# A convolution block: last product in four column tiles, its sum through DRAM, and the squares of queries and keys on GpSimd

## The chip, the core and the metric

The kernel runs on one core of one Trainium2 chip. The metric is device time in microseconds (us), the median of several runs. PE is TensorE, PEld its weight load, DVE is VectorE, ACT is ScalarE, POOL is GpSimd, SP is SyncE, which issues most of the DMAs here.

## The reference, cut to what matters

Three stages follow each other on x of 32 samples x 96 channels x 1024 positions: a convolution block (below, with C = 96, 8 heads of 12), causal attention with 6 heads of 16, and a feed-forward layer with quantized activations. Only the first stage and the projection of queries, keys and values that hangs on it are touched. `xs` is x after a group norm over 3 channels.

```python
xn = (xs - mu) / sqrt(var + EPS) * ln_g + ln_b
mid = silu(xn @ fc1_w + fc1_b) @ fc2_w + fc2_b          # 96 -> 384 -> 96
q, k, v = xs @ qkv_w                                    # per head of 12
q = q / norm(q);  k = k / norm(k)
attn = einsum('bhld,bhle->bhde', k, v)
o = 0.5 * v + 1.0 / pi * einsum('bhld,bhde->bhle', q, attn)
o = o / norm(o) + mid
x1 = x + (o @ proj_w + proj_b)
# then: t = tokens of x1;  q, k, v = ln(t) @ Wq, Wk, Wv   (causal attention)
```

## The kernel before

`prepare` loads and folds the weights once: `w["fc2"]` is fc2_w times proj_w, `w["out_bias"]` the bias of the sum. `conv_block` then takes the 32 samples one after the other through all its steps, as a pipeline: each engine has a `body(i, ...)` that in step i does one part for each of up to eight samples, `on(s)` meaning "the part that lags s samples". The order of the statements in each `body` is the order of the engine's work, and semaphores named after results tie the engines together. `_pipeline` unrolls the bodies. In one step:

- **TensorE** turns XN (L581), makes K'V (L588), waits for `a_ready`, makes the group mean G (L594), the QKV product of sample i-1 in eight tiles of 128 tokens x 384 (L604, two banks of `pq` in turn), the product M (L609), turns O-hat (L615), fc1's chunk 0 (L572, `hidden(i, 0)`), fc2 and proj of sample i-3 into `po` (L627, L631: two halves of 512 columns, K of 3 x 128 and 96), fc1's chunks 1 and 2 (L572), the attention projection of sample i-4 from X1 (L644, eight tiles), and the query product U (L651). `hidden` for chunk 1 waits until ScalarE has taken chunk 0 out of `pf` by its SiLU. K'V, M and G lie in `po`, which fc2 writes later.
- **ScalarE** squares O (L513), copies the turned XN (L516), takes roots (L519, L523, with a load of the root table), copies the QKV product out (L527, eight copies), squares its last 96 columns (L530) and queries and keys (L532), copies the turned O-hat (L535), rounds to bf16 (L539), roots again (L542, L546 and L548; these wait for the sums of the norms), loads the SiLU table and applies SiLU six times (L553), and takes the attention projection out: a copy (L561) and a square (L562) for each of eight tiles.
- **VectorE** sums a_squares (L388), masks the attention matrix (L391), sums O's squares and inverts the roots (L394, L398), copies G and makes the group variance (L402, L405), copies M (L409), scales queries and keys of sample i-5 to `a_qk` (L413, L416), makes the third bf16 part of sample i-6 (L421), sums the squares (L425, L426), scales XN and K-hat (L430 to L435), takes statistics of the next x (L442), adds x to fc2's result (L450, with x loaded a second time as XR), and at the end makes O (L462) and the normed x, XS (L471).
- **GpSimd** scales O (L482), waits until the packed rows of sample i-7 have been stored (`rows_stored`), makes the values' part (L489), a rest (L494), the scaled queries and values (L498), and a second rest (L503).
- **SP** issues in this order, first waiting for XS: x of the next sample (L365), x again (L368), the store of X1 (L371), the store of 1.5 MB packed rows (L374). All are on one queue.

The attention projection of sample i-4 reads X1 from SBUF one step after VectorE has made it. The feed-forward stage has a product in the tiled form that the change brings in (L1122).

Of the kernel before, what the change touches and what calls it, by code (L numbers as in the profile page):

```python
# [8 lines left out]
ALU = mybir.AluOpType  # L9
# [4 lines left out]
L = SIDE * SIDE  # L14
# [33 lines left out]
def _constants(nc, ctx):  # L48
# [15 lines left out]
    w["proj"] = sb("proj", [C, C])  # L64
    w["out_bias"] = sb("out_bias", [C, 1])
# [9 lines left out]
def prepare(nc, w, A):  # L75

    ctx = ExitStack()
    with ctx:
# [3 lines left out]
        def sem(name):  # L82
# [15 lines left out]
        projb = sb("projb", [C, 1])  # L98
# [17 lines left out]
            (w["proj"][:, :], A["L0_conv_proj_w"]),  # L116
# [13 lines left out]
            (projb[:, :], A["L0_conv_proj_b"].rearrange("(n a) -> n a", a=1)),  # L130
# [4 lines left out]
        with nc.Block() as block:  # L135
# [43 lines left out]
            def _(dve):  # L179
# [24 lines left out]
                link(dve.tensor_tensor(w["out_bias"][:, :], bank[4][0:C, 0:1], projb[:, :], ALU.add))  # L204
# [26 lines left out]
            def _(pe):  # L231
# [8 lines left out]
                pe.matmul(bank[4][0:C, 0:1], w["proj"][:, :], fc2b[:, :], start=True, stop=True)  # L240
# [7 lines left out]
                for k in range(CHUNKS):  # L248
                    pe.matmul(bank[0][:, k * C:(k + 1) * C], fc2_t[:, k * P:(k + 1) * P], w["proj"][:, :],
                              start=True, stop=True)  # L250
# [32 lines left out]
def conv_block(nc, w, x_in, x1, rows):  # L283
# [9 lines left out]
    with ExitStack() as ctx:  # L293
# [6 lines left out]
        XR = sb("x_again", [C, 2, L])  # L300
# [26 lines left out]
        OHT = sb("o_hat_t", [C, L])  # L327
        HT = sb("hidden_t", [P, 2, CHUNKS, L])
        AQKV = sb("a_qkv", [P, 2, TILES, 3 * C])
# [5 lines left out]
        AR1 = sb("a_rest", [P, TILES * HEADS, 2, HD])  # L335
        PK = sb("packed", [P, 2, TILES * HEADS, PACK], U32)

        def part(slot, n):
# [8 lines left out]
        x1_stored = [sem(f"x1_stored{i}") for i in range(2)]  # L347
        rows_stored = [sem(f"rows_stored{i}") for i in range(2)]
        names = ("bn_parts bn_done mv_ready g_done g_copied gn_var gn_std gn_scale xs_ready qkv_psum qkv_copied "
                 "squares norm_sums norm_roots norm_scales khat_ready xn_ready qv_ready kv_done a_ready m_done "  # L350
                 "m_ready xnt_psum xnt_ready fc1_psum hid_ready u_done o_ready o_squares o_sums o_roots o_scale "
                 "ohat_ready oht_psum oht_ready out_done x1_ready a_psum a_copied a_sums a_roots a_scale qk_ready "
                 "v_ready high_ready rest_ready mid_ready low_ready").split()
        S = {n: sem(n) for n in names}

# [3 lines left out]
        with nc.Block() as block:  # L359
            @block.sync  # L360
            def _(sp):
                def body(i, r, lap, on):
# [3 lines left out]
                    if on(3):  # L366
                        _above(sp.wait_ge, S["x1_ready"], i - 4)
                        sp.dma_start(XR[:, (r + 1) % 2, :], x_in[i - 3]).then_inc(xr_loaded[(r + 1) % 2], 16)  # L368
                    if on(4):
                        sp.wait_ge(S["x1_ready"], i - 3)  # L370
                        sp.dma_start(x1[i - 4], X1[:, r, :]).then_inc(x1_stored[r], 16)  # L371
                    if on(7):
# [3 lines left out]
                                     ).then_inc(rows_stored[(r + 1) % 2], 16)  # L376
                _pipeline(sp, body, BATCH, 8, 2, ahead=1)
                for r in range(2):
                    sp.wait_ge(x1_stored[r], 16 * (BATCH // 2))
                    sp.wait_ge(rows_stored[r], 16 * (BATCH // 2))  # L380

            @block.vector
            def _(dve):
                def body(i, r, lap, on):
                    q = (r + 1) % 2
                    if on(5):
                        dve.wait_ge(S["a_copied"], TILES * (i - 4))
# [4 lines left out]
                    if on(3):  # L392
# [5 lines left out]
                        dve.reciprocal(OI[:, :], OR[:, :]).then_inc(S["o_scale"], 1)  # L398
                    if on(0):
# [45 lines left out]
                    if on(3):  # L445
                        dve.wait_ge(S["out_done"], i - 2)
                        dve.wait_ge(xr_loaded[q], _dmas(lap, r, 3, 2))
                        _above(dve.wait_ge, x1_stored[q], _dmas(lap, r, 5, 2))
                        _above(dve.wait_ge, S["a_psum"], TILES * (i - 4))
                        dve.scalar_tensor_tensor(out=X1[:, q, :], in0=po[0:C, :], scalar=w["out_bias"][:, 0:1],  # L450
                                                 in1=XR[:, q, :], op0=ALU.add, op1=ALU.add).then_inc(S["x1_ready"], 1)
# [24 lines left out]
            def _(pool):  # L476
                def body(i, r, lap, on):
                    q = (r + 1) % 2
                    if on(3):
# [4 lines left out]
                                           _bcast(OI[:, :], 2, LIN_DIM), ALU.mult).then_inc(S["ohat_ready"], 1)  # L484
                    if on(5):
# [22 lines left out]
            def _(act):  # L508
                def body(i, r, lap, on):
# [14 lines left out]
                    if on(1):  # L524
# [7 lines left out]
                        act.activation(SQ[:, :, 0:2 * C], QKV[:, q, :, 0:2 * C], ACT.Square).then_inc(S["squares"], 1)  # L532
                    if on(3):
                        act.wait_ge(S["oht_psum"], i - 2)
                        act.activation(OHT[:, :], pt[0:C, :], ACT.Copy).then_inc(S["oht_ready"], 1)  # L535
# [31 lines left out]
            def _(pe):  # L567
# [7 lines left out]
                def body(i, r, lap, on):  # L575
# [10 lines left out]
                    if on(2):  # L586
# [741 lines left out]
```

## Time and profile before

| what | us |
|---|---|
| median of 3 runs | 3130.85 (3129.27 to 3132.96) |
| the profiled execution | 3126.59 |
| its span, first to last instruction | 3124.9 |
| convolution block within it | to about 1090 |
| 28 full samples of the block | 859.37, 30.69 each |

Busy times over the span: TensorE 2841.3 us, VectorE 2173.1, ScalarE 2052.4, GpSimd 1393.8. The shares are means over three stages with different limits. To read the change, one takes one sample of the block and follows each engine through it in the timeline view, where a gap is printed with the engine that ended it.

### The profile page before, as it was taken

The page shows a single profiled execution, that of the slowest core. Times are in us where ns is not written, and L with a number is a line of the kernel's source. Part 1 is how long each engine was busy: PE and PEld are TensorE (multiplying, and loading weights), DVE is VectorE, ACT ScalarE, POOL GpSimd, SP SyncE. Part 2 cuts the span into 40 slices and gives each one's busy share as a digit, 9 for nine tenths or more (in the row PEclk, how much of TensorE's full clock was granted, in tenths as well). Part 3 has the DMA queues.
Part 4 walks back from the last instruction along what each step waited for, and adds up shares of the span by engine and source line. Part 5 has one row for each costly group of instructions (what it writes and reads, how often), then busy time and mean ns, then how long its engine had stood idle before and what let it go on. Part 6 is the DMA issues. An engine that isn't in the chain of part 4 may idle for free. (4 is left out here: it accounts for less than half of the span.)

```text
span 3124.9 us, 85427 instructions
## 1 busy us (share of the span) xinstructions
PE 2841.3 (91%) x28774; PEld 1733.4 (55%) x28966; DVE 2173.1 (70%) x4403; ACT 2052.4 (66%) x3943; POOL 1393.8 (45%) x2063
## 2 busy tenths in 40 slices
PE   3899999999998589999999999999999979999883
PEld 2445455454544256666666666666666645555541
DVE  3565665656566378888898898889888935455542
ACT  2677777777776357777777777777777745666561
POOL 0143444444343444434444444443444413577778
PEclk9999999999999789999999999999999989999996
DMA  1113232322222367655556565565655523234434
GB/s 32 41 51 107 71 106 70 106 80 96 97 93 82 112 125 117 120 111 119 115 115 119 112 119 116 115 120 111 119 115 115 117 67 96 81 98 125 126 98 107
DMA packets 919803, 315.97 MB, mean 101 GB/s; under 512 B 848257, under 2 KB 904354, under 8 KB 919714
## 3 DMA queue, kind: packets, MB, share of 16 engines
q1 hardware_dynamic: 916258, 313.98, 42.4%
q8 instruction: 57, 0.93, 0.1%
q10 hardware_dynamic: 3456, 0.79, 0.1%
q14 instruction: 32, 0.26, 0.0%
HBM read 113.35 MB, written 99.88 MB: 68 GB/s over the span
## 5 line engine op out<-in xcount | busy, mean ns | idle before, releaser
L939 DVE TENSOR_REDUCE at_unit_max<-at_ps_queries 128x1 f32<-128x512 f32 (+3 forms) x2304 | 1121.1, 548 | 119.7 <-PE at_ps_queries L831 97.5
L905 ACT ACTIVATE at_probs<-at_ps_keys 128x512 f32<-128x512 f32 x1344 | 738.5, 596 | 244.7 <-PE at_ps_keys L845 216.7
L831 PE MATMUL at_ps_queries<-at_turned 96*128 96x512 bf16 (+3 forms) x2304 | 688.0, 330 | 64.3 <-DMA at_turned<-at_spread 31.8
L845 PE MATMUL at_ps_keys<-at_turned 128*128 128x128 bf16 (+3 forms) x3264 | 593.8, 268 | 2.9 <-ACT at_probs L905 2.4
L845 PEld LDWEIGHTS at_ps_keys<-at_turned 128*128 128x128 bf16 x3456 | 255.4, 97 | 241.1 <-ACT at_probs L905 122.6
L865 PE MATMUL at_ps_values<-at_probs,at_v 128*32 128x128 f32 x10752 | 373.4, 276 | 0.5 <-ACT at_probs L905 0.5
L799 POOL TENSOR_TENSOR at_tick<-at_one 128x1 f32<-128x1 f32 x192 | 37.1, 193 | 705.5 <-ACT at_diag_probs L905 460.2
L834 PE MATMUL at_ps_queries<-mask_queries,ident_bf 128*128 128x128 bf16 x1536 | 338.8, 221 | 0.0
L865 PEld LDWEIGHTS at_ps_values<-at_probs,at_v 128*32 128x32 f32 x10752 | 270.6, 109 | 42.3 <-ACT at_probs L905 1.3
L1189 POOL TENSOR_SCALAR ff_hidden<-ff_hidden 128x1024 f32<-128x1024 f32 x90 | 246.9, 2769 | 63.6 <-ACT ff_hidden L1147 63.6
L831 PEld LDWEIGHTS at_ps_queries<-at_turned 96*128 96x128 bf16 x2304 | 217.5, 98 | 100.7 <-DMA at_turned<-at_spread 32.9
L482 POOL TENSOR_TENSOR cb_o_hat<-cb_o,cb_o_scale 128x768 f32<-128x768 f32 x32 | 48.0, 1501 | 402.0 <-DVE cb_o_scale L398 402.0
L905 ACT ACTIVATE at_diag_probs<-at_ps_keys 128x512 f32<-128x512 f32 x384 | 208.5, 595 | 13.0 <-PE at_ps_keys L845 4.5
L801 POOL TENSOR_SCALAR_AFFINE_SELECT at_diag_probs<-at_diag_probs 128x1024 f32<-128x1024 f32 x192 | 209.6, 1091 | 0.0
L604 PE MATMUL cb_ps_qkv<-w_lin,cb_xs 96*128 96x384 f32 x512 | 198.9, 521 | 7.0 <-ACT cb_qkv L527 4.5
L644 PE MATMUL cb_ps_qkv<-w_attn,cb_x 96*128 96x384 f32 x512 | 198.2, 512 | 5.8 <-ACT cb_a_squares L562 4.3
L1122 PE MATMUL ff_ps_out<-ff_hidden,w 128*32 128x256 f32 x2160 | 138.7, 410 | 62.3 <-POOL ff_hidden L1189 23.6
L572 PE MATMUL cb_ps_hidden<-cb_xn_t,fc 96*128 96x512 f32 x384 | 185.7, 614 | 8.4 <-ACT cb_hidden_t L553 8.4
L834 PEld LDWEIGHTS at_ps_queries<-mask_queries,ident_bf 128*128 128x128 bf16 x1536 | 151.9, 99 | 72.5 <-issue 0.8
L462 DVE SCALAR_TENSOR_TENSOR cb_o<-cb_q_norm_v,cb_ps_hidden 128x768 f32<-128x768 f32 x32 | 30.5, 953 | 210.2 <-PE cb_ps_hidden L651 210.2
L627 PE MATMUL cb_ps_out<-cb_hidden_t,fc 128*96 128x512 f32 x384 | 176.6, 595 | 0.0
L1056 PE MATMUL ff_ps_hidden<-ff_xn_t,w 97*128 97x512 f32 x360 | 172.0, 600 | 1.1 <-ACT ff_xn_t L1154 1.1
(199 smaller groups left out, 4896.4 us busy)
## 6 DMA issues: line engine op xcount, KB each, us to landing
qkv_rows<-cb_packed SPq DMA_DIRECT2D x32, 1536.0 KB, 8.3
at_stacks<-qkv_rows SPq DMA_DIRECT2D x192, 256.0 KB, 3.2
cb_x<-in_x_dram SPq DMA_DIRECT2D x32, 384.0 KB, 3.7
cb_x_again<-in_x_dram SPq DMA_DIRECT2D x32, 384.0 KB, 4.5
x_after_conv<-cb_x SPq DMA_DIRECT2D x32, 384.0 KB, 5.0
attention_rows<-at_att SPq DMA_DIRECT2D x384, 32.0 KB, 2.1
ff_att_rows<-attention_rows SPq DMA_DIRECT2D x32, 384.0 KB, 3.7
ff_x<-x_after_conv SPq DMA_DIRECT2D x32, 384.0 KB, 4.7
```

What stands on the lines that cost most here:

```text
L572: pe.matmul(pf[:, a * BANK:(a + 1) * BANK], w["fc1"][:, k * P:(k + 1) * P], XNT[:, a * BANK:(a + 1) * BANK], start=True, stop=True).then_i ...
L604: pe.matmul(pq[:, (t % 2) * BANK:(t % 2) * BANK + 4 * C], XS[:, q, t * P:(t + 1) * P], w["w_lin"][:, :], start=True, stop=True).then_inc(S ...
L627: pe.matmul(po[0:C, half], w["fc2"][:, k, :], HT[:, q, k, half], start=(k == 0), stop=False)
L644: pe.matmul(pq[:, (t % 2) * BANK:(t % 2) * BANK + 4 * C], X1[:, r, t * P:(t + 1) * P], w["w_attn"][:, :], start=True, stop=True).then_inc( ...
L801: pool.affine_select(out=blocks, in_=blocks, compare_op=ALU.is_ge, fill=0.0, base=0, pattern=[[0, TILES], [1, P]], channel_multiplier=-1). ...
L831: mm = pe.matmul(pq[:, u % QBANKS, 0:n], QT[0:STACK, slot, qb * P:(qb + 1) * P], KT[0:STACK, slot, k0:k0 + n], start=True, stop=True)
L834: mm = pe.matmul(pq[:, u % QBANKS, n - P:n], w["ident_bf"][:, :], w["mask_queries"][:, :], start=False, stop=True, skip_group_check=True)
L845: mm = pe.matmul(pk[:, bank_k, c0:c0 + n * P], KT[:, slot, kb * P:(kb + 1) * P], QT[:, slot, q0 * P:(q0 + n) * P], start=(c0 == 0), stop=True,
L865: mm = pe.matmul(pv[row:row + VW, col:col + P], V[:, slot, kb, :], probs[:, c0:c0 + P], start=(v == 0), stop=True, skip_group_check=True)
L905: act.activation(probs, pk[:, (slot * NU + k) % KBANKS, :], ACT.Exp, scale=scale).then_inc(S["probs"], 1)
L939: dve.tensor_reduce(MX[:, r % 2, qb, k0 // BANK:k0 // BANK + 1], pq[:, u % QBANKS, 0:n], AX.X, ALU.max).then_inc(S["unit_max"], 1)
L1189: pool.tensor_scalar(Y1[:, s % SLOTS, k, :], Y1[:, s % SLOTS, k, :], LIMIT, None, ALU.min).then_inc(S["h_ready"], 1)
```

## The change

It does six things in the convolution block.

1. fc2 and proj go into `po` in four column tiles: tile g holds 32 channels (three blocks b of them in turn) and a quarter of the tokens, 256 columns; 4 K-chunks x 3 x 4 = 48 matmuls of 32 output rows. The bias becomes a 97th row of `w["proj"]` against a row of ones in OHT. The result lies as 128 partitions x 768.
2. VectorE's addition of x is a plain addition of 128x768 into X1Q. XR is loaded, and X1Q stored, in that layout, by four DMAs each. X1 (96x1024), which the attention projection reads, is loaded back from DRAM, issued behind the store of the rows, once the store of X1Q has landed.
3. The squares of queries and keys move from ScalarE to GpSimd, behind L482 and ahead of L489.
4. In TensorE's order, the wait for `a_ready`, G, and with it M come behind the QKV product. On VectorE the copy of M comes ahead of the copy of G and the group variance.
5. The attention projection is copied out whole (384 columns), and its squares are one operation of 128x768 behind the eight copies.
6. A root of one column, whose result isn't used, ends ScalarE's step.

```diff
@@ sync
-                        sp.dma_start(XR[:, (r + 1) % 2, :], x_in[i - 3]).then_inc(xr_loaded[(r + 1) % 2], 16)
+                        for q in range(4):
+                            sp.dma_start(XR[q * QP:(q + 1) * QP, (r + 1) % 2, :, :], quarters(x_in[i - 3])[q]
+                                         ).then_inc(xr_loaded[(r + 1) % 2], 16)
                     if on(4):
                         sp.wait_ge(S["x1_ready"], i - 3)
-                        sp.dma_start(x1[i - 4], X1[:, r, :]).then_inc(x1_stored[r], 16)
+                        for q in range(4):
+                            sp.dma_start(quarters(x1[i - 4])[q], X1Q[q * QP:(q + 1) * QP, r, :, :]
+                                         ).then_inc(x1_stored[r], 16)
                     if on(7):
...
+                    if on(4):
+                        sp.wait_ge(x1_stored[r], 4 * _dmas(lap, r, 4, 2))
+                        sp.dma_start(X1[:, r, :], x1[i - 4]).then_inc(x1_loaded[r], 16)
@@ vector
                     if on(5):
-                        dve.wait_ge(S["a_copied"], TILES * (i - 4))
+                        dve.wait_ge(S["a_squares"], i - 4)
...
+                    if on(2):
+                        dve.wait_ge(S["m_done"], i - 1)
+                        dve.tensor_copy(MM[:, :], M_).then_inc(S["m_ready"], 1)
                     if on(0):
...
                         dve.scalar_tensor_tensor(out=GV[:, 0:1], in0=GS[:, 0:1], scalar=GS[:, 0:1], in1=GS[:, 2:3],
                                                  op0=ALU.mult, op1=ALU.subtract).then_inc(S["gn_var"], 1)
-                    if on(2):
-                        dve.wait_ge(S["m_done"], i - 1)
-                        dve.tensor_copy(MM[:, :], M_).then_inc(S["m_ready"], 1)
...
                     if on(1):
-                        dve.wait_ge(S["squares"], 2 * i)
+                        dve.wait_ge(S["squares"], i)
                         dve.tensor_reduce(VS[:, :], SQ[:, :, 2 * C:3 * C], AX.X, ALU.add)
+                        dve.wait_ge(S["qk_squares"], i)
...
-                        dve.scalar_tensor_tensor(out=X1[:, q, :], in0=po[0:C, :], scalar=w["out_bias"][:, 0:1],
-                                                 in1=XR[:, q, :], op0=ALU.add, op1=ALU.add).then_inc(S["x1_ready"], 1)
+                        dve.tensor_tensor(X1Q[:, q, :, :].rearrange("p b t -> p (b t)"), po[:, 0:3 * QT],
+                                          XR[:, q, :, :].rearrange("p b t -> p (b t)"), ALU.add
+                                          ).then_inc(S["x1_ready"], 1)
@@ gpsimd, between L482 and L489
+                    if on(1):
+                        pool.wait_ge(S["qkv_copied"], 8 * i)
+                        _above(pool.wait_ge, S["norm_sums"], i - 1)
+                        pool.tensor_tensor(SQ[:, :, 0:2 * C], QKV[:, q, :, 0:2 * C], QKV[:, q, :, 0:2 * C], ALU.mult
+                                           ).then_inc(S["qk_squares"], 1)
@@ scalar
-                        act.activation(SQ[:, :, 0:2 * C], QKV[:, q, :, 0:2 * C], ACT.Square).then_inc(S["squares"], 1)
...
-                            act.activation(AQKV[:, r, t, :], pq[:, (t % 2) * BANK:(t % 2) * BANK + 3 * C], ACT.Copy)
-                            act.activation(ASQ[:, t, :], pq[:, (t % 2) * BANK + 3 * C:(t % 2) * BANK + 4 * C],
-                                           ACT.Square).then_inc(S["a_copied"], 1)
+                            act.activation(AQKV[:, r, t, :], pq[:, (t % 2) * BANK:(t % 2) * BANK + 4 * C], ACT.Copy
+                                           ).then_inc(S["a_copied"], 1)
+                        act.wait_ge(S["a_copied"], TILES * (i - 3))
+                        act.activation(ASQ[:, :, :], AQKV[:, r, :, 3 * C:4 * C], ACT.Square
+                                       ).then_inc(S["a_squares"], 1)
+                        act.activation(ROOT[:, :], w["eps"][:, 0:1], ACT.Sqrt)
@@ tensor
-                        pe.wait_ge(S["a_ready"], i - 1)
-                    if on(0):
-                        pe.wait_ge(S["mv_ready"], i + 1)
-                        pe.matmul(G_, w["group_mean"][:, :], MV[:, 0:3], start=True, stop=True).then_inc(S["g_done"], 1)
                     if on(1):
                         pe.wait_ge(S["xs_ready"], i)
...
+                    if on(2):
+                        pe.wait_ge(S["a_ready"], i - 1)
                     if on(0):
-                        pe.wait_ge(S["g_copied"], i + 1)
+                        pe.wait_ge(S["mv_ready"], i + 1)
+                        pe.matmul(G_, w["group_mean"][:, :], MV[:, 0:3], start=True, stop=True).then_inc(S["g_done"], 1)
...
-                        for a in range(2):
-                            half = slice(a * BANK, (a + 1) * BANK)
-                            for k in range(CHUNKS):
-                                pe.matmul(po[0:C, half], w["fc2"][:, k, :], HT[:, q, k, half], start=(k == 0),
-                                          stop=False)
-                            if a == 0:
+                        if on(0):
+                            pe.wait_ge(S["g_copied"], i + 1)
+                        for k in range(CHUNKS + 1):
+                            if k == CHUNKS:
+                                pe.wait_ge(S["ones_set"], 1)
                                 pe.wait_ge(S["oht_ready"], i - 2)
-                            mm = pe.matmul(po[0:C, half], w["proj"][:, :], OHT[:, half], start=False, stop=True)
+                            for b in range(3):
+                                for g in range(4):
+                                    chans, toks = slice(b * QP, (b + 1) * QP), slice(g * QT, (g + 1) * QT)
+                                    mm = pe.matmul(po[g * QP:(g + 1) * QP, b * QT:(b + 1) * QT],
+                                                   w["proj"][:, chans] if k == CHUNKS else w["fc2"][:, k, chans],
+                                                   OHT[:, toks] if k == CHUNKS else HT[:, q, k, toks],
+                                                   start=(k == 0 and b != 1), stop=(k == CHUNKS),
+                                                   skip_group_check=True)
...
                     if on(4):
+                        pe.wait_ge(x1_loaded[r], _dmas(lap, r, 4, 2))
```

## Rows read from the trace of the kernel before

**Rows 1.** The page's part 1: busy time, share of the span, instructions.
```profile
PE 2841.3 (91%) x28774; PEld 1733.4 (55%) x28966; DVE 2173.1 (70%) x4403; ACT 2052.4 (66%) x3943; POOL 1393.8 (45%) x2063
```
**Rows 2.** Windows: stretch, its length, busy time by engine, clock, DMA.
```profile
146.42:1005.79 859.37, 827.88 (x3136) 426.63 (x3135) 527.37 (x661) 617.73 (x1203) 370.00 (x140) 1.00 0.26 88
513.69:544.16 30.47, 29.46 (x114) 15.17 (x113) 19.18 (x24) 22.06 (x43) 12.88 (x5) 1.00 0.27 90
```
**Rows 3.** Timeline, TensorE: start, length, line, out<-in, shapes, count, [idle before <-releaser].
```profile
516.92 0.33 PE L594 MATMUL cb_ps_out<-cb_mean_var,group_mean 96*96 96x3 f32 x2 [0.84 <-DVE cb_attn_matrix L391]
...
523.19 0.33 PE L609 MATMUL cb_ps_out<-cb_attn_matrix,wq_t 96*96 96x96 f32 x2
...
525.96 2.74 PE L627 MATMUL cb_ps_out<-cb_hidden_t,fc 128*96 128x512 f32 x6
...
532.83 3.78 PE L572 MATMUL cb_ps_hidden<-cb_xn_t,fc 96*128 96x512 f32 x8
```
**Rows 4.** Timeline, ScalarE, the same sample.
```profile
523.39 0.49 ACT L527 ACTIVATE cb_qkv<-cb_ps_qkv 128x384 f32<-128x384 f32 x1 [0.16 <-PE cb_ps_qkv L604]
...
524.66 1.47 ACT L532 ACTIVATE cb_squares<-cb_qkv 128x1536 f32<-128x1536 f32 x1
...
531.76 1.27 ACT L553 ACTIVATE cb_hidden_t<-cb_ps_hidden,fc_bias 128x512 f32<-128x512 f32 x2
```
**Rows 5.** Timeline, VectorE, the same sample.
```profile
519.03 1.53 DVE L405 SCALAR_TENSOR_TENSOR cb_group_var<-cb_group_stats 96x1 f32<-96x1 f32 x1
...
523.96 1.76 DVE L416 TENSOR_TENSOR cb_a_qk<-cb_a_qkv,cb_a_scale 128x1536 f32<-128x1536 f32 x1
...
528.17 1.75 DVE L426 TENSOR_REDUCE cb_norm_sums<-cb_squares 128x128 f32<-128x1536 f32 x1
...
544.36 0.95 DVE L462 SCALAR_TENSOR_TENSOR cb_o<-cb_q_norm_v,cb_ps_hidden 128x768 f32<-128x768 f32 x1 [6.53 <-PE cb_ps_hidden L651]
```
**Rows 6.** Timeline, GpSimd, the same sample.
```profile
526.34 2.37 POOL L489 TENSOR_TENSOR cb_packed<-cb_a_qkv,cb_a_scale 128x768 f32<-128x768 f32 x1 [5.79 <-DMA qkv_rows<-cb_packed]
528.68 3.09 POOL L494 TENSOR_TENSOR cb_a_rest<-cb_a_qk,cb_packed 128x1536 f32<-128x1536 f32 x1
```
**Rows 7.** Windows, the feed-forward stage: the tiled product L1122, 72 records, alone.
```profile
2810.60:2814.64 4.04, 4.03 (x73) 2.24 (x73) 2.85 (x2) 3.00 (x3) 3.04 (x2) 1.00 0.76 215
```
**Rows 8.** Timeline, SP's issues: the row store, and four issues of 96 KB.
```profile
517.66 0.41 SPq L374 DMA_DIRECT2D qkv_rows<-cb_packed  x1
...
2812.96 2.30 SPq L1037 DMA_DIRECT2D ff_x_again<-x_after_attention  x4
```
**Rows 9.** Timeline, an early sample: VectorE, GpSimd, TensorE.
```profile
187.16 1.76 DVE L416 TENSOR_TENSOR cb_a_qk<-cb_a_qkv,cb_a_scale 128x1536 f32<-128x1536 f32 x1
188.84 3.03 DVE L421 TENSOR_TENSOR cb_packed<-cb_a_rest,cb_packed 128x1536 bf16<-128x1536 f32 x1
...
192.65 1.74 DVE L426 TENSOR_REDUCE cb_norm_sums<-cb_squares 128x128 f32<-128x1536 f32 x1
...
187.21 3.04 POOL L489 TENSOR_TENSOR cb_packed<-cb_a_qkv,cb_a_scale 128x768 f32<-128x768 f32 x1 [3.45 <-DVE cb_a_scale L413]
...
196.97 3.89 PE L572 MATMUL cb_ps_hidden<-cb_xn_t,fc 96*128 96x512 f32 x8 [0.77 <-ACT cb_hidden_t L553]
```
**Rows 10.** Timeline, past the last sample's QKV product: GpSimd, then VectorE.
```profile
1011.15 1.50 POOL L482 TENSOR_TENSOR cb_o_hat<-cb_o,cb_o_scale 128x768 f32<-128x768 f32 x1 [13.43 <-DVE cb_o_scale L398]
...
1011.32 2.95 DVE L416 TENSOR_TENSOR cb_a_qk<-cb_a_qkv,cb_a_scale 128x1536 f32<-128x1536 f32 x1
```
**Rows 11.** Timeline, TensorE behind two long waits, two of eight.
```profile
1012.71 1.94 PE L615 MATMUL cb_ps_turn<-ident,cb_o_hat 128*96 128x128 f32 x8 [3.77 <-POOL cb_o_hat L482]
...
1042.56 1.91 PE L615 MATMUL cb_ps_turn<-ident,cb_o_hat 128*96 128x128 f32 x8 [5.93 <-POOL cb_o_hat L482]
```
**Rows 12.** Windows behind such waits, the longest and the shortest of eight.
```profile
1012.70:1018.60 5.90, 5.89 (x13) 3.24 (x14) 4.51 (x2) 3.88 (x4) 4.14 (x2) 0.50 0.00 0
...
3074.10:3076.90 2.80, 2.80 (x28) 1.42 (x32) 0.83 (x1) 2.80 (x3) 2.80 (x2) 0.50 0.79 183
```

More of the change, by code:

```diff
@@ L63, in _constants @@
     w["fc2"] = sb("fc2", [P, CHUNKS, C])
-    w["proj"] = sb("proj", [C, C])
-    w["out_bias"] = sb("out_bias", [C, 1])
+    w["proj"] = sb("proj", [C + 1, C])
     w["w_attn"] = sb("w_attn", [C, 4 * C])
@@ L97, in prepare @@
         fc2b = sb("fc2b", [C, 1])
-        projb = sb("projb", [C, 1])
+        projb = sb("projb", [1, C])
         ones1 = sb("ones1", [C, P])
@@ L115, in prepare @@
             (w["w_lin"][:, 0:3 * C], A["L0_conv_qkv_w"]),
-            (w["proj"][:, :], A["L0_conv_proj_w"]),
+            (w["proj"][0:C, :], A["L0_conv_proj_w"]),
             (fc1_raw[:, :], A["L0_conv_fc1_w"]),
@@ L129, in prepare @@
             (fc2b[:, :], A["L0_conv_fc2_b"].rearrange("(n a) -> n a", a=1)),
-            (projb[:, :], A["L0_conv_proj_b"].rearrange("(n a) -> n a", a=1)),
+            (projb[:, :], A["L0_conv_proj_b"].rearrange("(a n) -> a n", a=1)),
             (w["bp"][:, :], A["L1_attn_bp"].rearrange("(n a) -> n a", a=1)),
@@ L203, in _ @@
                 link(dve.tensor_copy(fc2_t[:, :], bank[3][0:C, 0:HIDDEN]))
-                link(dve.tensor_tensor(w["out_bias"][:, :], bank[4][0:C, 0:1], projb[:, :], ALU.add))
+                link(dve.tensor_tensor(w["proj"][C:C + 1, :], bank[4][0:1, 0:C], projb[:, :], ALU.add))
                 link(dve.tensor_copy(w["w_attn"][:, :], bank[5][0:C, 0:4 * C]))
@@ L239, in _ @@
                     pe.transpose(bank[3][0:C, k * P:(k + 1) * P], fc2_raw[:, k, :], idn[:, :])
-                pe.matmul(bank[4][0:C, 0:1], w["proj"][:, :], fc2b[:, :], start=True, stop=True)
+                pe.matmul(bank[4][0:1, 0:C], fc2b[:, :], w["proj"][0:C, :], start=True, stop=True)
                 pe.matmul(bank[5][0:C, 0:4 * C], w["centre"][:, :], attn_raw[:, :], start=True, stop=True)
@@ L248, in _ @@
                 for k in range(CHUNKS):
-                    pe.matmul(bank[0][:, k * C:(k + 1) * C], fc2_t[:, k * P:(k + 1) * P], w["proj"][:, :],
+                    pe.matmul(bank[0][:, k * C:(k + 1) * C], fc2_t[:, k * P:(k + 1) * P], w["proj"][0:C, :],
                               start=True, stop=True)
@@ L299, in conv_block @@
         X = sb("x", [C, 2, L])
-        XR = sb("x_again", [C, 2, L])
+        XR = sb("x_again", [P, 2, 3, L // 4])
+        X1Q = sb("x1_quarters", [P, 2, 3, L // 4])
         X1 = sb("x1", [C, 2, L])
@@ L326, in conv_block @@
         XNT = sb("xn_t", [C, L])
-        OHT = sb("o_hat_t", [C, L])
+        OHT = sb("o_hat_t", [C + 1, L])
         HT = sb("hidden_t", [P, 2, CHUNKS, L])
-        AQKV = sb("a_qkv", [P, 2, TILES, 3 * C])
+        AQKV = sb("a_qkv", [P, 2, TILES, 4 * C])
         ASQ = sb("a_squares", [P, TILES, C])
@@ L335, in conv_block @@
         AR1 = sb("a_rest", [P, TILES * HEADS, 2, HD])
+        ROOT = sb("root_of_eps", [P, 1])
         PK = sb("packed", [P, 2, TILES * HEADS, PACK], U32)
@@ L347, in conv_block, with quarters @@
         x1_stored = [sem(f"x1_stored{i}") for i in range(2)]
+        x1_loaded = [sem(f"x1_loaded{i}") for i in range(2)]
         rows_stored = [sem(f"rows_stored{i}") for i in range(2)]
-        names = ("bn_parts bn_done mv_ready g_done g_copied gn_var gn_std gn_scale xs_ready qkv_psum qkv_copied "
-                 "squares norm_sums norm_roots norm_scales khat_ready xn_ready qv_ready kv_done a_ready m_done "
+        names = ("ones_set bn_parts bn_done mv_ready g_done g_copied gn_var gn_std gn_scale xs_ready qkv_psum qkv_copied "
+                 "squares qk_squares norm_sums norm_roots norm_scales khat_ready xn_ready qv_ready kv_done a_ready m_done "
                  "m_ready xnt_psum xnt_ready fc1_psum hid_ready u_done o_ready o_squares o_sums o_roots o_scale "
-                 "ohat_ready oht_psum oht_ready out_done x1_ready a_psum a_copied a_sums a_roots a_scale qk_ready "
+                 "ohat_ready oht_psum oht_ready out_done x1_ready a_psum a_copied a_squares a_sums a_roots a_scale qk_ready "
                  "v_ready high_ready rest_ready mid_ready low_ready").split()
         S = {n: sem(n) for n in names}
+        QP, QT = C // 3, L // 4
+        def quarters(dram):
+            return dram.rearrange("(b c) (q t) -> q c b t", c=QP, t=QT)
         def halves(ps):
@@ L383, in _ @@
             def _(dve):
+                dve.memset(OHT[C:C + 1, :], 1.0).then_inc(S["ones_set"], 1)
                 def body(i, r, lap, on):
@@ L531, in body @@
                                        ACT.Square).then_inc(S["squares"], 1)
-                        act.activation(SQ[:, :, 0:2 * C], QKV[:, q, :, 0:2 * C], ACT.Square).then_inc(S["squares"], 1)
                     if on(3):
                         act.wait_ge(S["oht_psum"], i - 2)
-                        act.activation(OHT[:, :], pt[0:C, :], ACT.Copy).then_inc(S["oht_ready"], 1)
+                        act.activation(OHT[0:C, :], pt[0:C, :], ACT.Copy).then_inc(S["oht_ready"], 1)
                     if on(5):
```

7 lines of the change are left out of this document (3 added, 4 removed).

## The prediction, made before the changed kernel was built or timed

> **What bounds the kernel now.** The page comes first: TensorE is busy for 91% of the span [rows 1], but the change touches only the convolution block, so that share has to be read again there. The windows view gives 28 samples from 146.42 to 1005.79 us, 859.37 us, or 30.69 us a sample, with the clock at full; TensorE works 29.46 of 30.47 us in one of them, VectorE 19.2, ScalarE 22.1, GpSimd 12.9 [rows 2]. So in this block TensorE sets the pace, and there is little to win besides its own work.
>
> I take the sample from 513.69 to 544.16 us and count times from its start, the turn of XN. TensorE waits 0.84 us for the attention matrix before the group mean (L594), starts the product M (L609) at 9.50, fc2 and proj at 12.27, and the second chunk of fc1 (L572) at 19.14 [rows 3]. ScalarE ends the copies of the QKV product at 10.19, squares queries and keys in 1.47 us, and starts the first two SiLUs, 1.27 us together, at 18.07 [rows 4]. VectorE starts "a_qk" (L416) at 10.27 and ends the sums of the norms (L426) at 16.23; at the end it waits 6.53 us for TensorE, so it isn't short of time over the sample [rows 5]. GpSimd waits 5.79 us for the rows of an earlier sample to leave, until 12.65 [rows 6].
>
> The point of the reading is that fc1's second chunk needs the first SiLU, the SiLU stands on ScalarE behind the roots of the norms, and these need L426. The first is done at 18.07+0.64 = 18.7, TensorE gets there at 19.14: **a slack of 0.4 us**. Anything that makes TensorE quicker before that point, or L426 later, becomes a TensorE wait.
>
> **The change, part by part.**
>
> *fc2 and proj in column tiles.* Now 16 records from 12.27 to 19.14, 6.87 us [rows 3]. The same form runs in the last stage: 72 records of 128x32 by 256 columns take 4.04 us to the next instruction [rows 7]. The change has 4 x 3 x 4 matmuls, 96 records: 4.04 x 96/72 = 5.4 us, and 5.4 to 5.8 with a turn into the form that the row doesn't show. It saves 1.1 to 1.5 us; I take 1.5.
>
> *G behind the QKV product, root table loaded ahead.* The 0.84 us wait goes, but TensorE then meets ScalarE, whose copies free the two banks. ScalarE's table load leaves the start of the sample; what is late next is VectorE's sum of O's squares. I take the copies 0.4 us earlier than before, that is to end at 9.77 (bounds 0 and 0.84). G's own 0.2 us now stands in front of M. M starts at 9.25, and TensorE would be ready for fc1's second chunk at 19.14-0.25-1.5 = **17.4**.
>
> *a_qkv copied whole, squared in one go.* The QKV product has such copies already (0.49 us each, [rows 4]); a gain of at most 0.2 us, taken as nothing. The dummy root at the end fills ScalarE time that was idle.
>
> *Squares of queries and keys on GpSimd.* It takes 1.47 us off ScalarE, which is not the bound, and puts 128x1536 with two inputs on GpSimd: 3.09 us by L494 [rows 6]. What matters is what else wants to run. GpSimd begins right behind the last copy, at 9.8. VectorE reaches L416 about 0.5 us later, since it now does MM, the copy of G and the group variance first. And the two engines do not run such operations side by side. At 1011.15 GpSimd starts L482; VectorE's L416, started at 1011.32, takes 2.95 us and ends at 1014.27, which is 1.62 us after GpSimd's end at 1012.65 [rows 10]. A 96x1 operation, L405, takes 1.53 us because it meets the 1.50 us of L482 [rows 5]. In the other order, at 187.21, GpSimd's L489 waits for L416 and ends 1.33 us behind it, and VectorE's L421, which came after, takes 3.03 us in place of 1.75 [rows 9]. They go one by one in the order in which they came. The Trainium skill, SBUF — State Buffer, section Who interferes with whom, states this as an exclusive lock between a VectorE operation with two SBUF inputs and a GpSimd operation that reads SBUF, held for the whole instruction. By that rule, with which the trace agrees, moving work to GpSimd takes as much from VectorE as it lasts; without it the sum would be rival 3.
>
> So: GpSimd squares 9.8 to 12.9. VectorE stands until then: L405, the reciprocal, L416 from 13.1.
>
> *Does GpSimd's L489 come ahead of L421?* It now asks at 12.65, when the rows have landed. The change puts six more issues ahead of the row store on SP. Four such issues take 2.30 us [rows 8], so the store leaves some 3.2 us later than at 3.97. The bytes ahead of it are the same and it had to queue behind them, so the landing moves by less: 13.0 to 14.6. L421 asks at 14.8. So L489 is first, as at 187.21. From L416's start to L426's end that sample took 7.23 us (187.16 to 194.39), and TensorE's fc1 began at 196.97, 2.58 us behind that [rows 9]. Now: 13.1+7.23 = 20.35 for L426, 20.35+2.58 = **22.9** for fc1's second chunk. TensorE waits 22.9-17.4 = 5.5 us. That same sample is the small model of it: L426 1.27 us late, TensorE idle 0.77 us.
>
> *The rest of the sample* is TensorE's own, from 532.83 to the next sample's start at 544.16, 11.33 us [rows 2, 3]: 22.9+11.3 = **34.2 us** at full clock.
>
> *The clock.* Every idle stretch of TensorE of 3.77 us or more since the first sample, eight of them, is followed by a granted clock of half, 1.2 GHz in place of 2.4: the shortest is 3.77, the nearest in length 5.93 [rows 11]. The clock stays there for 2.80 to 5.90 us after the restart, 4.5 in the mean of the eight [rows 12]. In 4.5 us it does 2.25 us of work. Some 0.3 of the loss falls into waits for ScalarE. I add **2.0 us** (bounds 0 and 2.9).
>
> *Sum through DRAM.* VectorE's sum becomes 128x768, and X1 is stored and loaded again. The load is issued behind the row store and lands by 13 to 17; the product that needs it starts at 26 or later. Cover: 9 us. Without it, each us late is a us more. Only the last sample has no cover: a store and a load, some 10 us, against a wait of about the same length that stands there now; I add 2 us for the end of the block. The bias row in proj costs nothing: 97 rows stream as 96.
>
> **The sum.** 34.2+2.0 = 36.2 against 30.69, +5.5 us a sample. Squares and L416 stand together in 28 samples: +155. With the end +2. The profiled execution took 3126.6 us around a span of 3124.9; the median of the three runs, 3130.85, is 4.3 above it, and I carry that over: 3130.85+157 = **3288 us**.
>
> **Rivals.**
> 1. *L489 stays behind L421*, as in most samples now, because the rows land after 14.8. Then L426 ends at 13.1+5.96 = 19.1, fc1 starts at 21.7, TensorE waits 4.3 us, still enough for half clock: 33.0+2.0 = 35.0, +4.3 x 28 = +120, 3253 us. For it: six more issues, smaller packets. Against: the landing would have to move by over 2.2 us.
> 2. *Order as forecast, but the clock stays up*: 34.2, +3.5 x 28 = +98, 3231 us; with rival 1 as well, 33.0, 3196. Against: eight of eight stretches.
> 3. *Faster: GpSimd's squares and VectorE run side by side.* L416 and L421 aren't held up, and L426 waits only for the squares: 10.4+1.7+1.7+0.9+1.7 = 16.4. fc1 starts at 19.0, where TensorE is ready at 17.4; the sample is 30.3 or less, and 29.9 if the copies come earlier: -0.4 to -0.8 a sample, 3109 to 3120 us. It decides as soon as the two don't exclude each other for this operation, whose two inputs are the same tile. Against: every overlap in rows 5, 9 and 10. A full gain, TensorE's 1.7 us a sample (3080 us), would need the slack of 0.4 to be over 2, too.
> 4. *Worse than forecast*: the half clock lasts through the attention product, or the reload of X1 comes after 26. Price 1 to 3 us a sample more, 3316 to 3370 us.
> 5. *No change*: column tiles bring nothing and the locks fall between; it needs two errors that cancel.
>
> **How the numbers follow.** Forecast 0.52, rival 1 0.14, rival 2 0.12, rival 3 0.09, rival 4 0.10, rival 5 0.03. Its own range is 3268 to 3312 (half clock 2.8 to 5.9 us). The range for 8 in 10 takes in rival 1, half of rival 2 and a bit of rival 4: 3205 to 3325. A difference below 0.2% (6 us) is about what can't be told from none here. Faster 0.08, within 0.2% 0.03, slower 0.89.
>
> **What the profile after would show.** A sample of 34 to 37 us in the block. TensorE's largest wait at L572 on ScalarE's SiLU, some 5.5 us, with the clock at half behind it. L416 starting after, or stretched to, the end of GpSimd's squares, and L421 at 3.0 us. The tiled product at 5.4 us for 96 records. The squares at 3.1 us on GpSimd, L530 alone on ScalarE. The prediction is wrong if L416 takes 1.76 us in the midst of the squares, if TensorE's wait before fc1's second chunk is below 3 us, or if the clock is full behind a wait of 5 us.

## The result, and the profile after

The changed kernel takes 3280.2 us (median of 4 runs, 3277.6 to 3283.2) against 3130.1 for the kernel before, on the same chips: a ratio of 1.0476, 95% interval 1.0462 to 1.0490. It is 4.8% slower. The forecast was 3288 us.

The page of the profile after, parts 1 and 2: busy time by engine, then TensorE's busy share and its granted clock in 40 slices of the span.

```profile
PE 2887.8 (88%) x31526; PEld 1770.3 (54%) x31526; DVE 2288.3 (70%) x4404; ACT 2029.1 (62%) x3719; POOL 1453.4 (44%) x2095
...
PE   3988878887888876999999999999999979899983
...
PEclk9989888998899887999999999999999988999996
```

The last two stages take as long as before within 1.3 us together. In the first 16 slices, the convolution block, TensorE has come down from nine tenths to eight, and its clock is no longer full. The windows view gives the 28 samples that answer to those of [rows 2], and then one stretch that begins where TensorE starts again behind its wait.

```profile
144.90:1157.96 1013.06, 847.19 (x5377) 462.85 (x5376) 638.82 (x661) 597.32 (x1008) 418.44 (x168) 0.91 0.30 86
...
672.05:678.90 6.85, 6.85 (x9) 2.81 (x10) 6.61 (x7) 2.58 (x4) 3.34 (x1) 0.52 0.00 0
```

1013.06/28 = 36.18 us a sample, against 30.69. These 28 samples hold 153.7 us of the span's 151.4 us of growth; the rest of the kernel gains 2.3 us. What TensorE waits for in those samples, from the waits view (total us, times, longest):

```profile
PE cb_ps_hidden L596 <- ACT cb_hidden_t L574: 139.3, 28, 5.2
PE cb_ps_qkv L624 <- ACT cb_qkv L549: 25.8, 28, 1.0
```

The first is new (before, such waits came to 2.3 us in all, in three samples): 5.0 us a sample in which TensorE waits for ScalarE's SiLU before fc1's second chunk. The second takes the place of the 0.84 us wait of [rows 3]. Now one sample, from 649.51 to 686.37 us, TensorE's timeline (start, length, line, shapes, count, idle before and what ended it):

```profile
649.51 1.04 PE L605 MATMUL cb_ps_turn<-ident,cb_xn 128*96 128x128 f32 x8
...
654.18 4.54 PE L624 MATMUL cb_ps_qkv<-w_lin,cb_xs 96*128 96x384 f32 x12 [0.92 <-ACT cb_qkv L549]
...
661.59 4.09 PE L656 MATMUL cb_ps_out<-cb_hidden_t,fc 128*32 128x256 f32 x72
665.50 1.48 PE L656 MATMUL cb_ps_out<-cb_o_hat_t,proj 97*32 97x256 f32 x24
672.05 6.97 PE L596 MATMUL cb_ps_hidden<-cb_xn_t,fc 96*128 96x512 f32 x8 [5.07 <-ACT cb_hidden_t L574]
```

The tiled product does what it should: 5.39 us from 661.59 to its end at 666.98, against 7.03 before by the same measure (6.87 to the start of the next product). Then TensorE stands for 5.07 us, and the eight records of fc1 that took 3.78 us in [rows 3] take 6.97: half clock. Why ScalarE is late stands in VectorE's and GpSimd's timelines of the same sample:

```profile
659.45 2.63 DVE L424 SCALAR_TENSOR_TENSOR cb_group_var<-cb_group_stats 96x1 f32<-96x1 f32 x1
662.02 0.18 DVE L429 RECIPROCAL cb_a_scale<-cb_a_var_roots 128x8 f32<-128x8 f32 x1
662.24 1.76 DVE L432 TENSOR_TENSOR cb_a_qk<-cb_a_qkv,cb_a_scale 128x1536 f32<-128x1536 f32 x1
663.91 3.02 DVE L437 TENSOR_TENSOR cb_packed<-cb_a_rest,cb_packed 128x1536 bf16<-128x1536 f32 x1
...
667.72 1.73 DVE L443 TENSOR_REDUCE cb_norm_sums<-cb_squares 128x128 f32<-128x1536 f32 x1
```
```profile
659.33 2.75 POOL L505 TENSOR_TENSOR cb_squares<-cb_qkv 128x1536 f32<-128x1536 f32 x1 [3.41 <-ACT cb_qkv L549]
662.79 2.53 POOL L511 TENSOR_TENSOR cb_packed<-cb_a_qkv,cb_a_scale 128x768 f32<-128x768 f32 x1 [0.72 <-DMA qkv_rows<-cb_packed]
```

GpSimd begins the squares 0.12 us before VectorE asks for L424, one column of 96 partitions. That one operation lasts 2.63 us and ends with the squares, at 662.08. L432 follows; L511 asks in its midst, goes next, and L437 stands behind it: 3.02 us in place of 1.75. The sums of the norms end at 669.45, which is 19.94 us into the sample; before it was 16.23.

### The profile page after: what moved, and what is told of

It reads as the page before. It is cut to its first block and busy times, and to the rows that moved or that the text cites. A ratio compares the mean times of both kernels' runs of the same rounds, so it can differ in the third digit from the quotient of the medians.

```text
span 3276.3 us, 91114 instructions
## 1 busy us (share of the span) xinstructions
PE 2887.8 (88%) x31526; PEld 1770.3 (54%) x31526; DVE 2288.3 (70%) x4404; ACT 2029.1 (62%) x3719; POOL 1453.4 (44%) x2095
## 5 line engine op out<-in xcount | busy, mean ns | idle before, releaser
L875 PE MATMUL at_ps_keys<-at_turned 128*128 128x128 bf16 (+3 forms) x3456 | 668.1, 275 | 2.7 <-ACT at_probs L935 2.3
L596 PE MATMUL cb_ps_hidden<-cb_xn_t,fc 96*128 96x512 f32 x384 | 257.8, 824 | 146.1 <-ACT cb_hidden_t L574 146.1
L499 POOL TENSOR_TENSOR cb_o_hat<-cb_o,cb_o_scale 128x768 f32<-128x768 f32 x32 | 48.0, 1500 | 486.2 <-DVE cb_o_scale L414 486.2
L596 PEld LDWEIGHTS cb_ps_hidden<-cb_xn_t,fc 96*128 96x128 f32 x384 | 92.0, 259 | 271.4 <-ACT cb_hidden_t L574 218.5
L574 ACT ACTIVATE cb_hidden_t<-cb_ps_hidden,fc_bias 128x512 f32<-128x512 f32 x192 | 128.4, 686 | 119.2 <-PE cb_ps_hidden L596 118.9
```

Source lines behind the costliest of these rows:

```text
L596: pe.matmul(pf[:, a * BANK:(a + 1) * BANK], w["fc1"][:, k * P:(k + 1) * P], XNT[:, a * BANK:(a + 1) * BANK], start=True, stop=True).then_i ...
L875: mm = pe.matmul(pk[:, bank_k, c0:c0 + n * P], KT[:, slot, kb * P:(kb + 1) * P], QT[:, slot, q0 * P:(q0 + n) * P], start=(c0 == 0), stop=True,
```

## The experiments

In each, the sample's length is the stretch over 28 samples divided by 28, and the ratio is to the kernel before, run beside it.

### Squares back on ScalarE, all else as changed

```diff
@@ gpsimd
-                    if on(1):
-                        pool.wait_ge(S["qkv_copied"], 8 * i)
-                        _above(pool.wait_ge, S["norm_sums"], i - 1)
-                        pool.tensor_tensor(SQ[:, :, 0:2 * C], QKV[:, q, :, 0:2 * C], ...
@@ scalar
+                        act.activation(SQ[:, :, 0:2 * C], QKV[:, q, :, 0:2 * C], ACT.Square
+                                       ).then_inc(S["qk_squares"], 1)
```

> The changed kernel with one part undone: ScalarE squares queries and keys again (1.47 us), everything else as changed. My theory: the loss is the squares on GpSimd alone, so L416's counterpart (L432) runs at once, from 10.5 us of the sample, in 1.76 us, the third part (L437) isn't held up, the sums of the norms end at 16.5, fc1's second chunk starts at 16.5+2.6 = 19.1 though TensorE is ready at 17.4, and the sample takes 19.1+11.3 = 30.4 us against 30.7 before: 3122 us, within 0.5% of the kernel before. The 1.5 us that the column tiles save show up as a wait of some 1.6 us ahead of fc1's second chunk, with the clock mostly full behind it. Rival: the sum through DRAM, the six more DMA issues or the column tiles themselves cost a good part; then it stays above 3180 us.

Measured: 3127.7 us, ratio 0.9985 (0.9975 to 0.9995). The windows view over its 28 samples, then VectorE's timeline:

```profile
141.32:1000.51 859.19, 790.69 (x5376) 438.63 (x5375) 510.97 (x661) 636.07 (x1036) 342.32 (x140) 0.98 0.35 101
...
609.70 0.21 DVE L424 SCALAR_TENSOR_TENSOR cb_group_var<-cb_group_stats 96x1 f32<-96x1 f32 x1
...
610.15 1.76 DVE L432 TENSOR_TENSOR cb_a_qk<-cb_a_qkv,cb_a_scale 128x1536 f32<-128x1536 f32 x1
611.83 1.75 DVE L437 TENSOR_TENSOR cb_packed<-cb_a_rest,cb_packed 128x1536 bf16<-128x1536 f32 x1
```

30.69 us a sample, the same as before the change. Undoing this one part takes the whole loss back, 5.5 us a sample; the column tiles, the sum through DRAM and the six more issues alone cost nothing that can be measured. (TensorE's wait in this run could hide a small cost; in the runs below that have no such wait the sample takes 28.9 us with all three in place.) They win little by themselves: TensorE is ahead by some 1.7 us and waits 41.9 us in 27 of the samples for the SiLU, 1.55 each. The forecast for this run, 30.4, was a little low. Most samples take 30.10 to 30.35 us, against 30.47 to 30.61 before, but in seven of the 28 the clock fell to half, in five of them behind a wait of only 1.5 us, and these take 31.85 to 34.18 us (clock 0.98 in the mean).

### TensorE kept at work through the wait

```diff
+                    if on(1) and on(5):
+                        for _ in range(11):
+                            pe.matmul(pt[0:C, 0:QT], w["ident"][:, 0:C],
+                                      w["fc2"][:, :, :].rearrange("p k c -> p (k c)")[:, 0:QT],
+                                      start=True, stop=True, skip_group_check=True)
                     if on(2):
                         hidden(i, 1)
```

> The changed kernel with eleven matmuls of 256 columns on constants, whose result nobody reads, put into TensorE's wait ahead of fc1's second chunk (11 x 0.43 = 4.7 us in a wait of 5.07). Nothing that anybody waits for comes sooner. My theory: the half clock is the consequence of the idle time and costs 2.3 us a sample (36.2 measured, against 22.5 until the chunk starts plus 11.3 at full clock), so the sample falls to 33.9 us and the kernel to 3280-65 = 3215 us, with a granted clock of 1.00 through the block: more work, less time. Rival: the time behind the wait is longer for another reason (ScalarE's SiLUs, the reload of X1); then it stays at 3280 us or rises.

Measured: 3210.2 us, ratio 1.0251 (1.0230 to 1.0273). TensorE's timeline in one sample, and the windows view over 28:

```profile
635.14 4.99 PE L664 MATMUL cb_ps_turn<-fc,ident 128*96 128x256 f32 x22
640.29 3.89 PE L596 MATMUL cb_ps_hidden<-cb_xn_t,fc 96*128 96x512 f32 x8 [0.15 <-ACT cb_hidden_t L574]
...
144.14:1091.97 947.83, 915.85 (x5993) 531.75 (x5991) 636.55 (x661) 597.33 (x1008) 420.34 (x168) 1.00 0.32 92
```

The chunk starts 22.55 us into the sample (617.74 to 640.29), as in the changed kernel (22.54). What follows takes 3.89 us in place of 6.97, and the sample 33.85 in place of 36.18. Eleven useless products make the kernel 70 us faster. So of the 150 us, 70 are the clock, which stays full as soon as TensorE doesn't stand still there, and 80 are the wait itself less what the tiles save.

### GpSimd's L511 behind L516

```diff
@@ gpsimd: the values' part (v, L511) moved behind the rest (AR1, L516)
```

> The changed kernel with one order changed on GpSimd: the values' part (L511, 1.5 us of work) comes behind the rest (L516) and not ahead of it. My theory says that L511, asking during L432, goes ahead of VectorE's L437 and holds it up by 1.27 us, and that the delay runs on into fc1's second chunk. Then L437 takes 1.75 us instead of 3.02, the sums of the norms end 1.27 us earlier, and the sample takes 34.9 us: 3280-36 = 3244 us. Rival: VectorE and GpSimd queue differently and another GpSimd operation takes the place, or L437 isn't on the path: 3280 us.

Measured: 3225.9 us, ratio 1.0300 (1.0280 to 1.0319); 959.97/28 = 34.28 us a sample. VectorE's timeline, and TensorE's wait:

```profile
635.33 2.63 DVE L424 SCALAR_TENSOR_TENSOR cb_group_var<-cb_group_stats 96x1 f32<-96x1 f32 x1
...
639.78 1.75 DVE L437 TENSOR_TENSOR cb_packed<-cb_a_rest,cb_packed 128x1536 bf16<-128x1536 f32 x1
...
PE cb_ps_hidden L596 <- ACT cb_hidden_t L574: 106.3, 28, 4.0
```

L424 is held up as before, L437 no longer is, and TensorE's wait falls by 33.0 us in 28 samples, 1.18 us each, close to the 1.27 us of the forecast. The sample gained more, 1.90 us. The rest is the clock: TensorE's busy time for the same 5377 records falls from 847.2 to 827.1 us, since 23 of the 28 half-clock stretches with the shorter wait lasted 3.4 us, where all of the changed kernel's had lasted 6.8 or more. I had taken the clock as unchanged; that term was missing, not the mechanism.

### GpSimd writes at that place, and reads nothing

```diff
-                        pool.tensor_tensor(SQ[:, :, 0:2 * C], QKV[:, q, :, 0:2 * C], QKV[:, q, :, 0:2 * C], ALU.mult
-                                           ).then_inc(S["qk_squares"], 1)
+                        pool.tensor_tensor(SQ[:, :, 0:1], QKV[:, q, :, 0:1], QKV[:, q, :, 0:1], ALU.mult)
+                        pool.memset(SQ[:, :, 1:2 * C], 1.0).then_inc(S["qk_squares"], 1)
```

> The changed kernel with GpSimd writing ones into the place of the squares of queries and keys (a memset behind a one-column product) instead of multiplying: same place in its order, same wait for it on VectorE, but it reads nothing from SBUF over its length. The squares are left out, so q and k aren't normed. My theory: VectorE's two-input operations are held up by what GpSimd reads; with the memset L424 takes 0.2 us and L432 1.76 us while GpSimd still works, the sample is 30.4 us and the kernel 3122 us, as if ScalarE squared. Rival: GpSimd at work as such holds VectorE up, or VectorE is late only because it waits for the squares: then L424 is stretched to the end of the memset, and the time lies between 3180 and 3280 us by the memset's length.

Measured: 3117.5 us, ratio 0.9949 (0.9933 to 0.9965); 860.95/28 = 30.75 us a sample. GpSimd's and VectorE's timelines:

```profile
609.10 1.37 POOL L506 MEMSET cb_squares<- 128x1528 f32 x1
```
```profile
609.02 0.22 DVE L424 SCALAR_TENSOR_TENSOR cb_group_var<-cb_group_stats 96x1 f32<-96x1 f32 x1
609.16 0.19 DVE L429 RECIPROCAL cb_a_scale<-cb_a_var_roots 128x8 f32<-128x8 f32 x1
609.47 1.76 DVE L432 TENSOR_TENSOR cb_a_qk<-cb_a_qkv,cb_a_scale 128x1536 f32<-128x1536 f32 x1
```

L432 starts at 609.47, while the memset runs until 610.47, and takes its usual 1.76 us. GpSimd at work doesn't hold VectorE up; GpSimd reading does. The memset is half as long as the squares, so the run says less about the total than about the overlap, but the overlap is plain. And VectorE still waits for GpSimd's result ahead of the sums of the norms, so that wait isn't what held it up. The Trainium skill, SBUF — State Buffer, section Who interferes with whom, makes this very exception for an operation that only writes, and the trace agrees.

### The squares on GpSimd alone, in the kernel before

The edit is the one of the change at GpSimd, ScalarE and VectorE's L425 and L426, on the kernel before.

> The kernel before with one part of the change alone: the squares of queries and keys on GpSimd, between L482 and L489. Theory: TensorE's order and the two halves of fc2 are as before, so it is ready for fc1's second chunk at 19.1. GpSimd's squares and VectorE's L416 are asked for within 0.1 us of each other, at 10.2 to 10.3. If the squares come first, L416 runs from 13.0, L489 ahead of L421, the sums of the norms end at 20.2, the chunk starts at 22.8 and the sample takes 34.1 us, with half clock behind a wait of 3.6 us some 35 to 36: 3250 to 3280 us. If L416 comes first, the squares stand between it and L421, the sums end at 19.0, the sample takes 33 us: 3195 to 3220 us. Rival: the change's new order on VectorE and its DMA issues ahead of the row store are needed for the loss; then this kernel stays within 1% of the kernel before.

Measured: 3249.6 us, ratio 1.0372 (1.0340 to 1.0404); 975.15/28 = 34.83 us a sample. VectorE, GpSimd and TensorE in one sample:

```profile
640.03 1.76 DVE L416 TENSOR_TENSOR cb_a_qk<-cb_a_qkv,cb_a_scale 128x1536 f32<-128x1536 f32 x1
641.71 4.30 DVE L421 TENSOR_TENSOR cb_packed<-cb_a_rest,cb_packed 128x1536 bf16<-128x1536 f32 x1
```
```profile
640.04 4.36 POOL L489 TENSOR_TENSOR cb_squares<-cb_qkv 128x1536 f32<-128x1536 f32 x1 [3.41 <-DVE cb_a_scale L413]
```
```profile
651.12 5.40 PE L577 MATMUL cb_ps_hidden<-cb_xn_t,fc 96*128 96x512 f32 x8 [2.05 <-ACT cb_hidden_t L558]
```

The order was the second of the two: L416 goes first, the squares stand behind it, and L421 behind the squares, 4.30 us. It was so in 27 of the 28 samples in which the two met, in nine of them with GpSimd's start recorded ahead. All but one of the 28 pairs of starts lie within 0.01 us of each other, and so close they don't tell who goes first. For that order I had forecast 33 us at full clock, and a kernel of 3195 to 3220 us: a miss. TensorE waits only 2.05 us, and still runs at half behind it, 5.40 us for what takes 3.78: 1.6 of the missing 1.8 us. Seven samples of 35.9 to 37.6 us, most with a longer stretch at half clock, lift the mean further. The squares on GpSimd alone thus cost 4.1 us a sample, so the rest of the change isn't needed for a loss; it makes this one 1.35 us larger (36.18 against 34.83). Most of that is the order: there the chunk starts at 22.54 us of the sample, here at 21.36.

### VectorE's two long operations into its idle time

```diff
@@ vector: L429 to L437 (a_scale, a_qk, third part) moved ahead of
                     if on(2):
                         dve.wait_ge(S["m_done"], i - 1)
                         dve.tensor_copy(MM[:, :], M_).then_inc(S["m_ready"], 1)
@@ scalar: the group root (L563) ahead of the bf16 copy (L560)
```

Squares on GpSimd as in the change:

> The changed kernel, squares still on GpSimd, with another order: VectorE scales a_qk and makes the third part (L429 to L437) ahead of the copy of M, in the 4.8 us in which it waits for it, and ScalarE takes the group root ahead of the bf16 copy. Then only the sums of the norms are left behind the squares: 12.6+0.1+1.7 = 14.4 for their end, 17.1 for the first SiLU, and TensorE is ready at 17.5. Theory: no wait there, the clock is full, the sample takes 17.5+11.3 = 28.8 us against 30.7 before, and the kernel 3131-1.9 x 28 = 3078 us: faster than both. Rival: GpSimd's work or VectorE's in-order waits bound the sample in another place (L416 held up by L482, the rest held up by the rows' landing); then it ends between 3090 and 3130 us.

Measured: 3079.1 us, ratio 0.9834 (0.9812 to 0.9856); 29.02 us a sample. TensorE, VectorE and GpSimd, and the windows view over 28 samples:

```profile
656.21 3.89 PE L596 MATMUL cb_ps_hidden<-cb_xn_t,fc 96*128 96x512 f32 x8 [0.30 <-ACT cb_hidden_t L574]
```
```profile
643.54 3.09 DVE L421 TENSOR_TENSOR cb_a_qk<-cb_a_qkv,cb_a_scale 128x1536 f32<-128x1536 f32 x1
646.56 1.75 DVE L426 TENSOR_TENSOR cb_packed<-cb_a_rest,cb_packed 128x1536 bf16<-128x1536 f32 x1
...
648.57 2.53 DVE L437 SCALAR_TENSOR_TENSOR cb_group_var<-cb_group_stats 96x1 f32<-96x1 f32 x1
...
651.89 1.73 DVE L443 TENSOR_REDUCE cb_norm_sums<-cb_squares 128x128 f32<-128x1536 f32 x1
```
```profile
144.97:957.66 812.69, 778.76 (x5377) 433.62 (x5375) 627.39 (x661) 598.98 (x1008) 415.24 (x168) 1.00 0.37 107
```

Nothing has been taken away. L421 is held up by L499 now (3.09 us), and the group variance by the squares (2.53), but both in time that VectorE had left, and only the sums stand behind the squares. TensorE's wait is 0.30 us and its clock full.

With the squares on ScalarE as well:

> As the run before, with the squares of queries and keys on ScalarE. Theory: both squares are done at 9.7+2.3 = 12.0, the sums of the norms end at 13.8, and TensorE sets the pace again: 28.8 us a sample, 3078 us, the same as with GpSimd's squares within 5 us; where the squares are made stops to matter once nothing that reads two tiles is queued behind them. Rival: ScalarE, now 1.5 us fuller, delays its copies and the time is 10 to 30 us above.

Measured: 3072.0 us, ratio 0.9819 (0.9793 to 0.9844); 28.86 us a sample. The intervals of the two ratios overlap: where the squares are made hardly matters any more. What is left of the 5.5 us is 0.16 us a sample, 7 us for the kernel, in favour of ScalarE. The windows view over the 28 samples:

```profile
141.42:949.39 807.97, 778.11 (x5377) 433.78 (x5375) 579.07 (x661) 632.24 (x1036) 344.48 (x140) 1.00 0.37 107
```

This is the fastest of the kernels here, some 60 us below the kernel before and 208 below the changed one.

The new order alone, on the kernel before:

> The kernel before with the new order of VectorE and ScalarE alone (L413 to L421 ahead of L409, the group root ahead of the bf16 copy); column tiles, sum through DRAM and the rest left out. Theory: the first SiLU comes some 2 us sooner, but TensorE, ready at 19.1, had only 0.4 us less than that to spare, so nothing is gained: 30.4 to 30.7 us a sample, 3120 to 3131 us. The slack alone brings nothing, the tiles alone nothing (shown by the squares back on ScalarE), the two together 1.9 us a sample. Rival: the earlier order gains by itself, over 20 us.

Measured: 3127.5 us, ratio 0.9985 (0.9974 to 0.9996); 30.53 us a sample:

```profile
146.94:1001.71 854.77, 825.56 (x3137) 426.13 (x3136) 565.77 (x661) 617.97 (x1203) 342.72 (x140) 1.00 0.26 89
```

The slack alone gives 0.15%, the change with its squares undone gives 0.15%, the two together 1.8%.

## Why the prediction was right

- **What bounds.** A slack of 0.4 us between TensorE and the first SiLU, with the sums of the norms behind it: right, and it is what the whole case turns on. With the squares back on ScalarE the sample stops at the first SiLU, with the new order alone at TensorE's own work, and neither gains more than 0.15%.
- **TensorE ready at 17.4.** Measured 17.47 (666.98-649.51). The tiles took 5.39 us where 5.4 was forecast, with no turn into or out of the form that shows; the copies of the QKV product end 9.74 us into the sample where 9.77 was forecast.
- **The squares shut VectorE out.** Right in each step: order, L424 stretched, L511 ahead of L437. One term was too large: the squares take 2.75 us, not the 3.09 of [rows 6], which was a subtraction of a bf16 part; mostly by this the chunk starts at 22.54 and not 22.9. And "in the order in which they came" holds for starts that are clearly apart, as the 0.05 to 0.13 us here. It didn't hold for L405 in [rows 5]: it starts 0.02 us ahead of L482 (519.03 and 519.05) and is still the one held up, while in the samples in which it starts 0.10 us ahead it takes its 0.21 us. The rows of the earlier sample landed 13.28 us into the sample, within the 13.0 to 14.6 forecast.
- **The clock.** Forecast 2.0 us a sample. TensorE's busy time for the same 5377 records is 847.19 us here and 778.76 in the run with the new order at full clock, 68.4/28 = 2.4 us; the filler run gives 36.18-33.85 = 2.3. The term was too small: behind the restart the half clock lasted 3.7 to 6.9 us, 5.4 in the mean, where 2.80 to 5.90 and 4.5 stood in the forecast. The reading was incomplete, too. The trace before has twelve waits of 3.77 us and more behind the first sample, not eight; half clock is there behind all twelve, but behind the four left out it lasted for 18 us or more. The chunk came 0.4 us early and the clock took 0.4 us more, so that 36.18 measured against 36.2 forecast is luck in its last digits; the mechanism is not.
- **The sum through DRAM.** Covered, as said. Only the last sample waits, by 4.92 us for the reload where 4.33 us stood before, and outside the 28 samples the kernel came out 2.3 us shorter in place of 2 longer: 1.5 ahead of them and 2.0 from their end to the attention stage (86.41 to 84.45 us), less 1.2 in the stages behind. No run separates what made the end shorter.
- **The sum.** 5.49 x 28 = 153.7 against 155. Rival 1 didn't come (the rows landed in time to let L511 in first), rival 2 fell with the clock, rival 3 with L424's 2.63 us, rival 5 with it. Of rival 4, the half clock did last longer than its range, but not through the attention product, and the reload isn't waited for in the 28 samples.

What the experiments corrected is the price of the half clock for shorter waits. In three runs the mechanism was as forecast and the clock's term was off: with L511 late it was taken as unchanged, with the squares back on ScalarE as next to nothing, and on the kernel before it was left out for the order that came.

## What to carry to other kernels

Before moving work to an idle engine, look at what else asks for the shared resource in that stretch: GpSimd was idle for 5.8 us there, and its 2.75 us of work with two inputs from SBUF held VectorE up for 2.4 us of them, in front of the one result that TensorE would need next. A faster step on the busiest engine pays only if what it meets next has slack; find that slack first, and make it by moving what nobody waits for into idle time. And a wait of TensorE costs more than its length when the clock falls behind it: here 5.0 us of wait brought 2.4 us more.

## What the runs showed that I had not expected

- The clock halves behind much shorter waits than those of 3.77 us and more that the forecast counted. On the kernel before with the squares moved, in which TensorE was else busy, each of the 27 waits (2.05 to 2.14 us, one of 3.46) was followed by half clock for 3.4 us or more. With the squares back on ScalarE, and a wait of 0.9 us earlier in each sample, five of the ten waits of 1.49 us were followed by it and none of the 14 of 1.38. The windows view of such a stretch in the run with the squares on ScalarE:

```profile
619.40:622.80 3.40, 3.40 (x5) 1.24 (x5) 3.15 (x4) 1.37 (x2) 3.40 (x2) 0.50 0.00 0
```

- The trace before had shown this already. TensorE waits 1.96 us before 2762.72 and 1.96 us before 2862.57, and the two stretches behind differ:

```profile
2762.86:2766.28 3.42, 3.42 (x36) 1.72 (x35) 1.80 (x2) 1.64 (x2) 3.42 (x2) 0.50 0.68 181
2862.57:2866.50 3.93, 3.93 (x72) 2.24 (x72) 1.94 (x2) 1.79 (x2) 3.93 (x2) 1.00 0.66 181
```

So for waits of about 2 us the length alone doesn't tell; no run here shows what does.

- GpSimd multiplies an fp32 tile of 128x1536 by itself in 2.75 us. L494 ([rows 6]) takes 3.09 for as many elements, but subtracts a bf16 part from an fp32 tile, so the price of one doesn't stand for the other; which of the differences makes the 0.34 us isn't shown.
- An operation of VectorE on one column of 96 partitions is held up for as long as any: 2.63 us for 0.21 us of work. A small operation with two inputs from SBUF costs as much as a large one if it meets GpSimd at the wrong time, so such ones are worth moving too.
